# Attention stage of a small language-model kernel: scores in pairs of banks with one exponential, two banks for row maxima, value and denominator batches in halves

## What is computed

```
qkv = layernorm(h) @ w_qkv.T + b_qkv       # 32 query heads, 8 key/value heads, head size 32
q, k = apply_rope(q), apply_rope(k)
scores = einsum('bhqd,bhkd->bhqk', q, k) / sqrt(32)
scores = where(causal, scores, -1e20)
out = einsum('bhqk,bhkd->bhqd', softmax(scores), v)
```

## Time and profile before

| | us |
|---|---|
| median of 3 runs | 4025.11 |
| lowest and highest | 4018.99, 4042.11 |
| the profiled execution's own time | 4027.74 |
| its span | 4025.9 |
| mean granted clock of PE | 0.969 of full |
| busy: PE, PEld | 3776.8, 2433.5 |
| busy: DVE, ACT, POOL | 2292.9, 1626.7, 1589.7 |

### The profile page before, as it was taken

How to read it: one execution, slowest core, us unless ns; L and a number is a source line. 1 busy time by engine, 2 the same in 40 slices (tenths; PEclk the granted TensorE clock), 3 DMA queues, 4 the chain that set the end, 5 groups by cost and what they waited for, 6 DMA issues and landing times. The chain is left out here.

```text
span 4025.9 us, 69672 instructions
## 1 busy us (share of the span) xinstructions
PE 3776.8 (94%) x22272; PEld 2433.5 (60%) x22272; DVE 2292.9 (57%) x3912; ACT 1626.7 (40%) x3068; POOL 1589.7 (39%) x525
## 2 busy tenths in 40 slices
PE   2889888899999999999999999999999779999999
PEld 2777777655555555555555555555555248888887
DVE  3666656676566566566566566566566144443443
ACT  2222222155555555555555555555555521010110
POOL 5222330045544544544544544545544513232322
PEclk9999999799999999999999999999999979999999
DMA  8877785411111111111111111111110243334432
GB/s 242 209 182 193 202 200 133 97 44 47 33 46 47 33 46 47 33 46 47 33 46 47 33 46 47 33 46 47 33 46 25 70 138 94 93 87 94 90 96 65
DMA packets 240124, 325.95 MB, mean 81 GB/s; under 512 B 62795, under 2 KB 139595, under 8 KB 239859
## 3 DMA queue, kind: packets, MB, share of 16 engines
q1 hardware_dynamic: 221426, 255.22, 23.7%
q0 software_dynamic: 18432, 67.12, 7.6%
HBM read 223.67 MB, written 97.52 MB: 80 GB/s over the span
## 5 line engine op out<-in xcount | busy, mean ns | idle before, releaser
L714 DVE TENSOR_REDUCE mpart<-mx_ps 128x1 f32<-128x512 f32 (+3 forms) x2560 | 1455.1, 606 | 841.4 <-PE mx_ps L769 455.3
L672 ACT ACTIVATE probs<-st_ps 128x512 f32<-128x512 f32 (+3 forms) x2560 | 1297.7, 533 | 1093.6 <-PE st_ps L798 535.7
L656 POOL TENSOR_TENSOR sums<-probs 128x2048 f32<-128x2048 f32 (+1 forms) x320 | 1182.6, 3696 | 1256.8 <-PE den_ps L827 1171.3
L795 PE MATMUL st_ps<-qs,k_score 98*128 98x512 f32 (+3 forms) x2560 | 1087.2, 428 | 31.2 <-issue 25.3
L766 PE MATMUL mx_ps<-k_max,qs 96*128 96x512 f32 (+3 forms) x2560 | 985.4, 393 | 14.5 <-POOL consts_r L647 14.1
L795 PEld LDWEIGHTS st_ps<-qs,k_score 98*128 98x128 f32 x2560 | 482.1, 189 | 814.5 <-ACT probs L672 659.6
L810 PE MATMUL o_ps<-probs,vs 128*32 128x512 f32 (+3 forms) x5120 | 606.9, 546 | 0.0
L766 PEld LDWEIGHTS mx_ps<-k_max,qs 96*128 96x128 f32 x2560 | 495.1, 195 | 48.2 <-POOL consts_r L647 14.3
L202 POOL DMA_INDIRECT hbuf<-in_tok_table,idx x128 | 194.1, 1517 | 352.3 <-ACT xn L233 231.2
L1030 POOL TENSOR_TENSOR h<-h,bb 128x1024 f32<-128x1024 f32 x32 | 105.1, 3283 | 543.2 <-DVE xn_c L1128 543.2
L386 PE MATMUL qk_ps<-x_hi,w_hi 128*128 128x512 f32 x640 | 259.7, 406 | 51.2 <-ACT rotation L245 31.8
(11 more groups left out here) (103 smaller groups left out, 3819.9 us busy)
## 6 DMA issues: line engine op xcount, KB each, us to landing
qs<-q_hi_scratch SPq DMA_DIRECT2D x128, 256.0 KB, 4.5
h_scratch<-hbuf SPq DMA_DIRECT2D x32, 512.0 KB, 3.5
q_hi_scratch<-rot_hi SPq DMA_DIRECT2D x64, 256.0 KB, 2.6
q_lo_scratch<-rot_lo SPq DMA_DIRECT2D x64, 256.0 KB, 3.3
qs<-q_lo_scratch SPq DMA_DIRECT2D x64, 256.0 KB, 5.5
o_scratch<-o_sb SPq DMA_DIRECT2D x64, 256.0 KB
o_in<-o_scratch SPq DMA_DIRECT2D x32, 512.0 KB, 4.4
o_in<-recip_scratch SPq DMA_DIRECT2D x128, 128.0 KB, 7.9
```

Of the source, the lines that this page charges most:

```text
L656: nc.gpsimd.tensor_tensor(sums[:, p % SUM_SLOTS, :, j * P:CT], a, b, ALU.add).then_inc(sum_done, 1)
L672: nc.scalar.activation(probs[:, s % SLOTS, h, j * P:CT], st_ps[:, u % SCORE_BANKS, 0:CT - j * P], ACT.Exp, scale=float(HD) ** -0.5).then_i ...
L714: nc.vector.tensor_reduce(mpart[:, h * TPC + t, kc:kc + 1], mx_ps[:, n % MAX_BANKS, 0:w], AX, ALU.max).then_inc(max_done, 1)
L795: mm = nc.tensor.matmul(st_ps[:, u % SCORE_BANKS, 0:w], k_score[0:M_ROW + 2, kt * P:(kt + 1) * P], qs[c][0:M_ROW + 2, h, j * P:CT], start= ...
```

## The change

The same eight banks are dealt anew: scores take two slots of two banks, one slot per pair of heads, maxima take two banks instead of four. PE writes the scores of two heads one behind the other and signals once; ScalarE takes one exponential over both banks (1024 columns where there were two of 512). A step has two halves: two scores, the first half of the step's entries, a value part; then the same again with the denominators behind it. The values lag by one step instead of two and are split at column 384: the part below it in the first half, the last 128 columns in the second. The denominators of a pair are split too, the first half at the end of one step, the second at the end of the next, so their first half comes one step sooner than before. SP and GpSimd wait for the same events in the new count. All other parts are the same.

```diff
-NU = NS * GROUP
+NU = NS * GROUP // 2
...
-SCORE_BANKS, MAX_BANKS = 2, 4
-VALUE_LAG, DEN_LAG = 2, 4
+SCORE_SLOTS, MAX_BANKS = 2, 2
+VALUE_LAG, DEN_LAG = 1, 4
+VALUE_SPLIT = 3 * P
...
-        st_ps = ctx.enter_context(nc.psum_tensor("st_ps", [P, SCORE_BANKS, CT], F32))
+        st_ps = ctx.enter_context(nc.psum_tensor("st_ps", [P, SCORE_SLOTS, 2, CT], F32))
         mx_ps = ctx.enter_context(nc.psum_tensor("mx_ps", [P, MAX_BANKS, CT], F32))
         o_ps = ctx.enter_context(nc.psum_tensor("o_ps", [P, CT], F32))
...
-            def exps(unit, pair, s, h):
-                u, j = s * GROUP + h, STEPS[s][2]
-                act.wait_ge(st_ready, unit + u + 1)
-                if h == 0 and s % 2 == 0:
+            def exps(unit, pair, s, half):
+                j = STEPS[s][2]
+                act.wait_ge(st_ready, unit + s * 2 + half + 1)
+                if half == 0 and s % 2 == 0:
                     act.wait_ge(den_done, pair + s // 2 + 1)
...
-                nc.scalar.activation(probs[:, s % SLOTS, h, j * P:CT], st_ps[:, u % SCORE_BANKS, 0:CT - j * P], ACT.Exp,
-                                     scale=float(HD) ** -0.5).then_inc(exp_done, 1)
+                nc.scalar.activation(probs[:, s % SLOTS, 2 * half:2 * half + 2, j * P:CT],
+                                     st_ps[:, half, :, 0:CT - j * P], ACT.Exp, scale=float(HD) ** -0.5
+                                     ).then_inc(exp_done, 1)
 
             def take_o(g, step, c):
                 act.wait_ge(pv_done, step + LAST_OF[c] + 1)
@@ -685,10 +687,10 @@
...
-            def scores(g, unit, s, h):
+            def scores(g, unit, s, first_head):
 
                 c, kt, j = STEPS[s]
-                u, w = s * GROUP + h, CT - j * P
+                w = CT - j * P
                 diagonal = kt >= c * TPC
-                if s in FIRST_OF and h == 0:
+                if s in FIRST_OF and first_head == 0:
                     pe.wait_ge(m_rows, 32 * (g * QC + c + 1))
                     pe.wait_ge(k_score_loaded[c], LOAD * (g + 1))
-                if not (is_first(g) and u < SCORE_BANKS):
-                    pe.wait_ge(exp_done, unit + u - (SCORE_BANKS - 1))
-                mm = nc.tensor.matmul(st_ps[:, u % SCORE_BANKS, 0:w], k_score[0:M_ROW + 2, kt * P:(kt + 1) * P],
-                                      qs[c][0:M_ROW + 2, h, j * P:CT], start=True, stop=not diagonal)
-                if diagonal:
-                    mm = nc.tensor.matmul(st_ps[:, u % SCORE_BANKS, 0:P], identr, mkq, start=False, stop=True)
+                if not (is_first(g) and s == 0):
+                    pe.wait_ge(exp_done, unit + s * 2 + first_head // 2 - 1)
+                for h in range(first_head, first_head + 2):
+                    mm = nc.tensor.matmul(st_ps[:, h // 2, h % 2, 0:w], k_score[0:M_ROW + 2, kt * P:(kt + 1) * P],
+                                          qs[c][0:M_ROW + 2, h, j * P:CT], start=True, stop=not diagonal)
+                    if diagonal:
+                        mm = nc.tensor.matmul(st_ps[:, h // 2, h % 2, 0:P], identr, mkq, start=False, stop=True)
                 mm.then_inc(st_ready, 1)
...
-            def values(g, unit, s):
+            def values(g, unit, s, part):
 
                 c, kt, j = STEPS[s]
-                pe.wait_ge(exp_done, unit + GROUP * (s + 1))
-                if s in FIRST_OF:
+                if part == 0:
+                    pe.wait_ge(exp_done, unit + 2 * (s + 1))
+                if s in FIRST_OF and part == 0:
                     pe.wait_ge(v_loaded[c], 16 * (g + 1))
...
-                for h in range(GROUP):
-                    mm = nc.tensor.matmul(o_ps[h * HD:(h + 1) * HD, j * P:CT], vs[:, kt, :],
-                                          probs[:, s % SLOTS, h, j * P:CT], start=s in FIRST_OF, stop=s in LAST_OF)
-                mm.then_inc(pv_done, 1)
-
-            def denominators(g, pair, p):
+                lo, hi = ((j * P, VALUE_SPLIT), (max(j * P, VALUE_SPLIT), CT))[part]
+                if lo < hi:
+                    for h in range(GROUP):
+                        mm = nc.tensor.matmul(o_ps[h * HD:(h + 1) * HD, lo:hi], vs[:, kt, :],
+                                              probs[:, s % SLOTS, h, lo:hi], start=s in FIRST_OF and part == 0,
+                                              stop=s in LAST_OF and part == 1)
+                if part == 1:
+                    mm.then_inc(pv_done, 1)
...
-                pe.wait_ge(sum_done, pair + p + 1)
-                if opening and not (is_first(g) and c == 0):
-                    pe.wait_ge(den_copied, g * QC + c)
-                if diagonal:
+                alone = (j * P, (j + 1) * P) if diagonal else (0, 0)
+                half = (j * P + CT) // 2 if diagonal else CT // 2
+                if part == 0:
+                    pe.wait_ge(sum_done, pair + p + 1)
+                    if opening and not (is_first(g) and c == 0):
+                        pe.wait_ge(den_copied, g * QC + c)
+                    if diagonal:
+                        for h in range(GROUP):
+                            nc.tensor.matmul(den_ps[h * HD:(h + 1) * HD, alone[0]:alone[1]], ones[:],
+                                             probs[:, 2 * p % SLOTS, h, alone[0]:alone[1]], start=opening, stop=False)
+                lo, hi = ((alone[1], half), (half, CT))[part]
+                if lo < hi:
                     for h in range(GROUP):
-                        nc.tensor.matmul(den_ps[h * HD:(h + 1) * HD, j * P:(j + 1) * P], ones[:],
-                                         probs[:, 2 * p % SLOTS, h, j * P:(j + 1) * P], start=opening, stop=False)
-                at = (j + 1) * P if diagonal else 0
-                for h in range(GROUP):
-                    mm = nc.tensor.matmul(den_ps[h * HD:(h + 1) * HD, at:CT], ones[:],
-                                          sums[:, p % SUM_SLOTS, h, at:CT], start=False, stop=closing)
-                mm.then_inc(den_done, 1)
-
-            def lagging_values(g, unit, s):
+                        mm = nc.tensor.matmul(den_ps[h * HD:(h + 1) * HD, lo:hi], ones[:],
+                                              sums[:, p % SUM_SLOTS, h, lo:hi], start=False,
+                                              stop=closing and part == 1)
+                if part == 1:
+                    mm.then_inc(den_done, 1)
...
-                if k % 2 == 0:
-                    return
                 if k >= 0:
-                    denominators(g, pair, k // 2)
+                    denominators(g, pair, k // 2, k % 2)
                 elif not is_first(g):
-                    denominators(g - 1, pair - PAIRS, (k + NS) // 2)
+                    denominators(g - 1, pair - PAIRS, (k + NS) // 2, k % 2)
...
                 for s in range(NS):
                     entries = entries_in(s, first, last)
-                    for h in range(GROUP):
-                        scores(g, unit, s, h)
-                        for more, n in entries[len(entries) * h // GROUP:len(entries) * (h + 1) // GROUP]:
+                    for part in range(2):
+                        scores(g, unit, s, 2 * part)
+                        for more, n in entries[len(entries) * part // 2:len(entries) * (part + 1) // 2]:
                             give(g + more, ring + more * NE, n)
-                        if h == GROUP // 2 - 1:
-                            lagging_values(g, unit, s)
+                        lagging_values(g, unit, s, part)
                     lagging_denominators(g, pair, s)
```

More of the change, by code:

```diff
@@ L687, in group @@
                 for s in range(NS):
-                    for h in range(GROUP):
-                        exps(unit, pair, s, h)
+                    for half in range(2):
+                        exps(unit, pair, s, half)
                         k = s - DEN_LAG - 1
-                        if h == 0 and k % NS in LAST_OF and not (first and k < 0):
+                        if half == 0 and k % NS in LAST_OF and not (first and k < 0):
                             take_den(pair if k >= 0 else pair - PAIRS, LAST_OF.index(k % NS))
@@ L816, in denominators @@
+                if part == 1:
+                    mm.then_inc(pv_done, 1)
+            def denominators(g, pair, p, part):
                 c, kt, j = STEPS[2 * p]
                 diagonal, opening, closing = kt >= c * TPC, 2 * p in FIRST_OF, 2 * p + 1 in LAST_OF
-                pe.wait_ge(sum_done, pair + p + 1)
-                if opening and not (is_first(g) and c == 0):
-                    pe.wait_ge(den_copied, g * QC + c)
-                if diagonal:
-                    for h in range(GROUP):
-                        nc.tensor.matmul(den_ps[h * HD:(h + 1) * HD, j * P:(j + 1) * P], ones[:],
-                                         probs[:, 2 * p % SLOTS, h, j * P:(j + 1) * P], start=opening, stop=False)
@@ new lines, in denominators, with lagging_values @@
+                lo, hi = ((alone[1], half), (half, CT))[part]
+                if lo < hi:
```

(22 more changed lines are left out.)

6 lines of the change are left out of this document (3 added, 3 removed).

## The result

The changed kernel takes **4427.0 us** (median of 4 runs, 4397.1 to 4449.2) against 4029.0 for the kernel before on the same chip: ratio 1.098, 95% interval 1.091 to 1.106. The forecast was 4208 us, 4105 to 4300: the sign is right, 219 us are missing. From its profiled execution (span 4447.4 us), these are the waits of the weight loader and of PE from 1000 to 2900 us (waiter, releaser: total us, times, longest); the earlier trace rows has them for the kernel before, from 1000 to 2800 us.

The account below looks back on a forecast made before the run. PE's queue was taken to bound part B. Terms of -46, +88, +102, +29 and +10 sum to +183 us on the profiled 4027.7 us, 4211 us, or 4208 us by the median; range 4105 to 4300 us.

Parts of the forecast that it names:

- (a): Score pairs with one exponential of 1024 columns: PE's real waits for exponentials go, -46 us.
- (b): Split value and denominator batches: entries into the column tiles rise from 60 to 76 per group, +88 us.
- (c): Two banks for maxima instead of four: PE waits for VectorE's reductions, 6.6 us a group, +102 us.
- (e): The first maxima, ahead of any score, wait with two banks and fuller first-group steps: 5 to 20 us, taken +10.
- (d): The loop's branch: PE's stall grows by 1.1 to 1.8 us and the clock falls nearly every time, +29 us.
- evenly: Spreading the batches evenly buys nothing against the added entries, since nothing but PE's own order waits there.
- Only the batches: Rival, chance 0.17: VectorE keeps up on two banks, (c) falls to some 10 and (e) to 5: 4114 us.
- Faster: Rival, chance 0.05: exponential waits are real in more places, costing PE more than 14.3 us a group; example 3953 us.
- No net change: Rival, chance 0.04: the split lets PE skip waits priced at nothing, (c) and (d) nearly vanish: about 4040 us.
- Waits that spread: Rival, chance 0.13: held maxima delay their next loads, plain half steps lose too, (c) grows by some 80: 4290 us.
- Instruction-bound tiles: Rival, chance 0.05: each of 6656 added tile matmuls costs 18 ns, 120 us more: 4328 us.

Follow-up runs that it names:

- run 4: The changed kernel with its loop over groups written out on every engine, so no branch between groups: 4140.4 us, 1.025 times before.
- run 6: The changed kernel unrolled, with 24 register operations on PE ahead of each of the last 14 groups, meant as a pause that did not come: 4142.2 us.
- run 7: The changed kernel unrolled, with 56 register operations on PE ahead of each of the last 14 groups, meant as a pause that did not come: 4141.9 us.
- run 13: The kernel before, with its group loop unrolled and otherwise untouched: 3977.1 us, 0.986 times before.
- run 12: The kernel before with three banks for scores and three for maxima, and its group loop unrolled too: 3929.2 us, 0.974 times before.
- run 3: The kernel before with split value and denominator batches only; single scores and four maxima banks stay: 4240.8 us, 1.050 times before.
- run 2: The changed kernel with its value and denominator batches whole again; score pairs and two maxima banks stay: 4273.8 us, 1.057 times before.
- run 9: The changed kernel with whole batches in steps 0 to 11 and 36 to 39, around the branch, split elsewhere: 4297.4 us, 1.066 times before.
- run 1: The kernel before with two banks for maxima in place of four and nothing else: 4191.3 us, 1.039 times before.
- Run 5: The changed kernel with only SyncE's last loads of a group put behind its wait for the last value batch: 4381.1 us, 1.088 times before.
- run 10: The changed kernel unrolled, with PE waiting ahead of step 0 of each group for three small chained DMAs, a pause without a branch: 4376.5 us, 1.083 times before.
- run 14: The changed kernel with batches whole in steps 12 to 35 and split in steps 0 to 11 and 36 to 39: 4406.2 us, 1.094 times before.
- run 8: The kernel before with three banks for scores and three for maxima in place of two and four: 3989.6 us, 0.990 times before.

## Why the prediction was wrong

The unrolled kernels split the price in two. As shares of before's time, the changed kernel stands at 1.0981 with its branch and 1.0270 without (mean of runs 4, 6, 7), the kernel before at 1 and 0.9862 (run 13). Of 4029 us, the change without a branch costs (1.0270 - 0.9862) x 4029 = **164 us**, where terms (a) to (c) and (e) gave 154. The branch cost 56 us before and costs 287 now: **+231 us**, where term (d) gave 29. The forecast failed on (d). That the 164 lie so near the 154 is partly luck: (a) to (c) came to less than their 144 and (e) to more than its 10, as shown below.

- **(a)** held: the 1024-column exponential takes 1.026 us (1.02 forecast). The waits were removed by other means in run 12: 147.3 - 144.3 = 3.0 us a group against run 13, with one maxima bank less, where 2.9 was forecast.
- **(b)** was priced too high, and one sentence of it is false, that "evenly" buys nothing. The split alone costs 3.6 us a group (run 3), not 5.5. In the changed kernel it even gains 1.9 (a first pass of 155.8 us against 157.7 in run 2): whole batches leave half steps with nothing between two pairs of maxima, and with two banks the loader's waits on mpart double (167 and 171 us in 1900, runs 2 and 9, against 84.9, run 4).
- **(c)** held: two maxima banks alone cost 6.3 us a group (run 1), where 6.6 was worked out. In run 4 the loader's waits are 84.9 x 155.7 / 1900 = 7.0 us a group, which is its idle time and not what PE lost; the longest was 1.1 instead of 0.8.
- **(a) to (c)** together: a steady group takes 155.7 instead of 147.3 us unrolled, 8.4 more; forecast 144 / 15.5 = 9.3. Taken alone they make -3.0 + 3.6 + 6.3 = 6.9, so 1.5 us a group comes of their meeting.
- **(d)** is the step that failed: "The stall grows by 1.1 to 1.8 ... and the clock will fall nearly every time, 8 more". PE's pauses at the 13 taken branches, from the last matmul's start to the next score's, grew from 2.5 to 6.5 us in the mean, by 3.9 instead of 1.6: 51 us for 21. I had held the branch's own duration fixed. But half a batch of values, half of one of denominators and a held maximum now stand between a group's last score and the branch, while SyncE's loads wait for that score alone and so run ahead of the branch. Run 5 gives 2.5 of the 2.7 us back; runs 1, 2 and 3, each with a part of that work, lie between (4.09, 4.96 and 5.12 us). The other 180 us are what is left, and are put down to the clock, priced at 8. The profiled executions agree: over the groups of the loop, what their lengths exceed the unrolled ones by, less the pauses, is some 25 us before and 227 after, for 31 and 542 us at half clock outside the pauses. I took the 1.7 us seen behind one branch as the price of a fall. It was the price of a fall among whole batches. Among split ones, with the narrow steps behind the pause, the clock stays down for up to 65 us (runs 3, 10 and 14 have them; whole ones, in runs 1, 2, 8 and 9, never over 17 us behind a branch): terms (b) and (d) are not independent, and were added.
- **(e)** was too small. The first score came 12 us later, as forecast (10), but the first group, with the same narrow steps at its start, takes 193 instead of 154 us unrolled, 30 more than the 8 of any group; 48 us of it are at half clock. So some 42 us for 10, and of the 164 some 122 are left for (a) to (c), forecast at 144.

The rivals: *Only the batches* is excluded by run 1, where two maxima banks cost 6.3 us a group; *Faster* by runs 12 and 13, where the exponential waits are worth 3.0 us a group and not over 14.3; *No net change* by the 164 us that stay without a branch. Of *Waits that spread* the runs show nothing (7.0 us a group of the loader's waits). *Instruction-bound tiles* is excluded by the same 164 us and by run 3. So is the 166 us that the page TensorEngine Tiling (Array Packing) of the Trainium skill led to, under Instruction Overhead: by that overhead per matmul the unrolled pair would lie an estimated 320 us apart. None of my rivals let the clock be the price. The Trainium skill's page TensorE: Matmul & The Clock Gate, in its Part 1 on the clock gate, puts the penalty of the ramp, which it tells of a kernel's start, at under 1% of a typical kernel span. Here the clock falls behind the branches too, and the 180 us are 4% of the span; the measurement decides.

Open: why the same pause brings 14 us behind one group and 61 behind another (run 10), and what in the split batches holds the clock down, their width, their number of entries or their short idle gaps. Run 5 moved only the loads and the branch became shorter; that what queues behind them is the fetch of its own instructions is argued, not shown. The Trainium skill's page Runtime: NRT & Kernel Launch, under Instruction fetch mechanics, says that a taken branch out of the prefetched code waits for a DMA that fetches its target, which would fit; no run here shows that fetch.

## What to carry to other kernels

Where a trace shows the clock falling at one place, ask what the edit puts around that place: a price read there holds only for the work that stands there now. Unroll both kernels once, or otherwise take the pause away, and the static price and the pause's price come apart in two runs. And ask of a bank what its fewer users would lose: here a third bank for scores, taken from maxima, did what the pairs were to do, and two taken cost 6.3 us a group (run 1).

## What was not expected of the hardware

- TensorE stayed at 1.2 GHz for 65 us with PE busy 60 of them, behind a 6 us pause, and for 61 us behind a pause of 2.1 us, with split batches around both. It returned within 21 us where full-width steps followed a 4.0 us pause.
- A taken loop branch on PE took 3.3 to 7.5 us over all runs. With PE's code unchanged it took 6.3 us in the median when 256 KB loads were issued just ahead of it, and 3.8 when they were issued behind it.
- Unrolling 14 groups brought no stall of its own: part B's window in run 12 has PE busy 2307.75 of 2310 us.
